# Attention weights of a graph layer: relu on ScalarE and one fused VectorE pass in place of two passes, and one broadcast row per head

## What is computed

```python
h = relu(layernorm(x))
ht = (h @ W).reshape(N, 4, 512).transpose(1, 0, 2)
src, dst = einsum("hnd,hd->hn", ht, a_src), einsum("hnd,hd->hn", ht, a_dst)
e = leaky_relu(src[:, :, None] + dst[:, None, :], 0.01) + adj_mat[None]
x = x + einsum("hij,hjd->hid", softmax(e, axis=-1), ht).mean(axis=0)
```

## Time and profile before

| | us |
|---|---|
| three runs | 2653.58, 2651.89, 2648.78 |
| median | 2651.89 |
| span of the profiled execution, first to last instruction | 2651.3 |
| PE busy in the span | 2503.3 |
| DVE busy in the span | 2309.6 |
| first matmul of the attention (L1226) starts at | 556.36 |

### The profile page before, as it was taken

The page is one execution under the profiler, slowest core; times in us unless marked ns, Lnnn a source line. Parts: engine busy times, 40 slices in busy tenths (PEclk is TensorE's granted clock), DMA queues, the critical chain, the costliest instruction groups (busy, mean ns, idle before and its releaser), DMA issues.

```text
span 2651.3 us, 46261 instructions
## 1 busy us (share of the span) xinstructions
PE 2503.3 (94%) x12326; PEld 1243.7 (47%) x12326; DVE 2309.6 (87%) x3220; ACT 1188.3 (45%) x1837; POOL 267.7 (10%) x206
## 2 busy tenths in 40 slices
PE   4899898759999999999999999999999999999997
PEld 1344346724444444444444444444444444444686
DVE  8998777479889998899888998888989899889796
ACT  5433344544444444454344553344544444444453
POOL 4105401310001000010001100010000100001000
PEclk8999998579999999999999999999999999999999
DMA  5443334420002100121001210022000210001000
GB/s 205 164 151 110 112 115 153 131 111 8 8 28 85 43 8 8 44 79 39 1 8 58 65 40 8 0 70 85 8 8 12 79 63 4 4 14 48 25 1 9
DMA packets 77246, 146.71 MB, mean 55 GB/s; under 512 B 4347, under 2 KB 12389, under 8 KB 76516
## 3 DMA queue, kind: packets, MB, share of 16 engines
q1 hardware_dynamic: 77156, 145.76, 17.2%
HBM read 131.99 MB, written 13.75 MB: 55 GB/s over the span
## 4 chain that ended last, share of the span: by engine, by line
PE 54%; DVE 17%; issue 6%; DVEq 3%; ACT 0%; ACTq 0%; POOLq 0%; POOL 0%
PE z_ps L1226 43%; PE o_ps L1250 10%; DVE t_reg L1140 5%; DVE ao_reg L1112 4%; DVE t_reg L1130 4%; DVE x_reg L1119 2%; DVE hl_reg L1097 1%; DVEq L1130 1%; PE c_ps L1241 1%; DVEq L1181 0%; DVE z_reg L1149 0%; DVEq L1119 0%; DVEq L1097 0%; ACT z_reg L1054 0%; DVEq L1128 0%
## 5 line engine op out<-in xcount | busy, mean ns | idle before, releaser
L1226 PE MATMUL z_ps<-hl_reg,h_reg 128*128 (+2 forms) x8736 | 1768.9, 365 | 55.9 <-DVE hl_reg L1097 40.2
L1226 PEld LDWEIGHTS z_ps<-hl_reg,h_reg 128*128 (+1 forms) x8736 | 855.2, 98 | 966.1 <-issue 44.7
L1042 ACT ACTIVATE hl_reg<-t_reg (+2 forms) x364 | 362.6, 996 | 870.4 <-PE z_ps L1226 485.8
L1130 DVE SCALAR_TENSOR_TENSOR t_reg<-ring_reg,vv,t_reg 128x512 f32 (+3 forms) x728 | 504.8, 736 | 7.7 <-issue 7.7
L1028 ACT ACTIVATE t_reg<-ring_reg,vv 128x512 f32 (+3 forms) x728 | 461.3, 681 | 29.4 <-DVE credits L1086 15.3
L1097 DVE TENSOR_TENSOR hl_reg<-t_reg,hl_reg (+2 forms) x364 | 417.4, 1147 | 31.8 <-ACT hl_reg L1042 31.1
L1140 DVE TENSOR_TENSOR t_reg<-t_reg,x_reg (+3 forms) x364 | 416.6, 1144 | 0.0
L1112 DVE TENSOR_TENSOR ao_reg<-ao_reg,t_reg 128x1024 f32<-128x1024 f32 (+1 forms) x336 | 384.7, 1145 | 0.0
L602 PE MATMUL z_ps<-t_reg,h_reg 128*128 (+2 forms) x1456 | 309.1, 373 | 53.5 <-DVE t_reg L384 47.2
L1250 PE MATMUL o_ps<-w_reg,z_reg 128*128 128x512 f16 x1248 | 273.9, 379 | 0.6 <-DVE z_reg L1149 0.6
L602 PEld LDWEIGHTS z_ps<-t_reg,h_reg 128*128 (+1 forms) x1456 | 144.6, 100 | 217.0 <-issue 61.3
(11 more groups left out here) (107 smaller groups left out, 855.8 us busy)
## 6 DMA issues: line engine op xcount, KB each, us to landing
ring_reg<-adjT_in SPq DMA_DIRECT2D x78, 512.0 KB, 3.7
x_reg<-adjT_in SPq DMA_DIRECT2D x78, 512.0 KB, 3.7
ring_reg<-rows_dram SPq DMA_DIRECT2D x24, 512.0 KB, 3.8
t_reg<-x_in SPq DMA_DIRECT2D x13, 512.0 KB, 4.2
x_dram<-x_reg SPq DMA_DIRECT2D x13, 512.0 KB, 4.7
ao_reg<-x_dram SPq DMA_DIRECT2D x6, 1024.0 KB, 5.6
out_dram<-ao_reg SPq DMA_DIRECT2D x6, 1024.0 KB
w_reg<-W_in SPq DMA_DIRECT2D x5, 1024.0 KB, 7.7
```

What stands on the lines that cost most here:

```text
L1042: nc.scalar.activation(hl_ring[:, g % HL_RING, 0, :, 0:W], t_ring[:, g % T_RING, :, 0:W], ACT.Copy).then_inc(hi_ready, 1)
L1130: nc.vector.scalar_tensor_tensor(out=tu, in0=u_bc[:, h, 1, 0:W], scalar=vv4[:, 1, h, bass.ds(p * 2 + u, 1)], in1=tu, op0=ALU.mult, op1=ALU ...
L1226: mm = nc.tensor.matmul(z_ps[:, k, 0:W], hk[hs], hl_ring[:, r, ps, u, 0:W], start=first and u == 0 and n == 0, stop=last and u == 1 and n ...
```

## The change

With C = U1 / U0 one value of i per head is enough: the weight is, up to a factor per i that cancels in the softmax, max(V1 C, V0) E = (relu(V1 C - V0) + V0) E. ACT does relu(V1 C - V0) with a per-partition scale and a per-partition bias, DVE adds V0 and multiplies by E in one scalar_tensor_tensor for each half. The pass L1140 is gone. The wait for the mask (`e_ready`) moves ahead of the first of these two. `p_ready` counts halves. `rows` has 5 rows in place of 9, and the broadcast load of a head is one row (256 KB) in place of two (512 KB). The factor 2^15 that the rows carried now goes into V0 and V1, so the rows no longer wait for a scaling pass on DVE (L886) before they are transposed; two small passes on V0, V1 and -V0 stand in its place.

```diff
@@ start of the stage
-                nc.vector.tensor_tensor(uu4[:, :, 0], qq3, lk3, ALU.subtract).then_inc(s_uarg, 1)
-                nc.vector.scalar_tensor_tensor(out=uu4[:, :, 1], in0=qq3, scalar=SLOPE, in1=lk3,
-                                               op0=ALU.mult, op1=ALU.subtract).then_inc(s_uarg, 1)
+                nc.vector.scalar_tensor_tensor(out=cc3, in0=qq3, scalar=SLOPE, in1=lk3,
+                                               op0=ALU.mult, op1=ALU.subtract).then_inc(s_carg, 1)
...
-                dve.wait_ge(s_uexp, 1)
-                nc.vector.tensor_scalar(rows[:, 0:2 * H * NT], rows[:, 0:2 * H * NT], PS, None,
-                                        ALU.mult).then_inc(s_rows, 1)
+                link(dve, nc.vector.tensor_scalar(vv[:, 0:2 * H * NT], vv[:, 0:2 * H * NT], PS, None, ALU.mult))
+                link(dve, nc.vector.tensor_scalar(vv4[:, 2], vv4[:, 0], -1.0, None, ALU.mult))
...
-                pe.wait_ge(s_rows, 1)
+                pe.wait_ge(s_cexp, 1)
+                pe.wait_ge(mt_red, len(max_groups))
@@ ACT, t1
                     for u in range(2):
-                        nc.scalar.activation(t_ring[:, g % T_RING, u, 0:W], u_bc[:, h, 0, 0:W], ACT.Copy,
-                                             scale=vv4[:, 0, h, bass.ds(p * 2 + u, 1)]).then_inc(t1_ready, 1)
+                        nc.scalar.activation(t_ring[:, g % T_RING, u, 0:W], c_bc[:, h, 0:W], ACT.Relu,
+                                             bias=vv4[:, 2, h, bass.ds(p * 2 + u, 1)],
+                                             scale=vv4[:, 1, h, bass.ds(p * 2 + u, 1)]).then_inc(t1_ready, 1)
@@ DVE, step
+                    if h == 0:
+                        dve.wait_ge(e_ready, b * PAIRS + p + 1)
                     for u in range(2):
                         dve.wait_ge(t1_ready, g * 2 + u + 1)
                         tu = t_ring[:, g % T_RING, u, 0:W]
-                        nc.vector.scalar_tensor_tensor(out=tu, in0=u_bc[:, h, 1, 0:W],
-                                                       scalar=vv4[:, 1, h, bass.ds(p * 2 + u, 1)], in1=tu,
-                                                       op0=ALU.mult, op1=ALU.max).then_inc(stt_done, 1)
+                        nc.vector.scalar_tensor_tensor(out=tu, in0=tu, scalar=vv4[:, 0, h, bass.ds(p * 2 + u, 1)],
+                                                       in1=e_blk[:, bass.ds(p * 2 + u, 1), 0:W]
+                                                       .rearrange("p o i -> p (o i)"),
+                                                       op0=ALU.add, op1=ALU.mult).then_inc(p_ready, 1)
                     if before:
                         lo_part(*before)
                     if e_of(b, h, p):
                         subtract_max(*e_of(b, h, p))
-                    dve.wait_ge(stt_done, g * 2 + 2)
-                    if h == 0:
-                        dve.wait_ge(e_ready, b * PAIRS + p + 1)
-                    nc.vector.tensor_tensor(tp, tp, e_blk[:, bass.ds(p * 2, 2), 0:W], ALU.mult).then_inc(p_ready, 1)
                     if before:
                         accumulate(*before)
```

More of the change, by code:

```diff
@@ L673, in gnn_kernel @@
         rows_out = sem("rows_out")
-        u_in = [sem(f"u_in{h}") for h in range(H)]
+        c_in = [sem(f"c_in{h}") for h in range(H)]
         e_in = [sem(f"e_in{p}") for p in range(PAIRS)]
@@ L736, in _ @@
                 load_max(sp, 0)
-                load_u(sp, 0, 0)
+                load_c(sp, 0, 0)
                 for p in range(EARLY, PAIRS):
@@ L740, in _ @@
                 for h in range(1, H):
-                    load_u(sp, 0, h)
+                    load_c(sp, 0, h)
                 load_x1(sp, 0)
@@ L783, in _ @@
                     nc.scalar.activation(vv4[:, q], dn3, ACT.Exp, scale=f).then_inc(s_vv, 1)
-                act.wait_ge(s_uarg, 2)
-                nc.scalar.activation(rows[:, 0:2 * H * NT], rows[:, 0:2 * H * NT], ACT.Exp).then_inc(s_uexp, 1)
+                act.wait_ge(s_carg, 1)
+                nc.scalar.activation(cc3, cc3, ACT.Exp).then_inc(s_cexp, 1)
                 for a in range(2):
```

51 lines of the change are left out of this document (24 added, 27 removed).

## The result

| | before | after |
|---|---|---|
| median, us | 2650.34 (4 runs, 2647.98 to 2653.58) | 2618.63 (4 runs, 2617.20 to 2618.89) |
| ratio, with its 95% interval | | 0.9879 [0.9865, 0.9893] |
| span of the profiled execution | 2651.3 | 2616.7 |
| DVE busy | 2309.6 | 1953.4 |
| ACT busy | 1188.3 | 1246.3 |

The kernel before has a fourth run here, 2647.98, beside the three listed above. The change makes the kernel 1.2% faster. 2616.5 was forecast, 2618.63 measured.

A forecast was written before the change was run, and what follows sets the result against it. PE bounds most stretches, so only its excess over its floor counts: 19.9 + 10.5 + 3.5 - 0.4 + 1.85 = 35.35 us off the span of 2651.3 gives 2616.0, forecast median 2616.5 us, range 2612 to 2629.

The forecast's parts named there:

- The bound: Full stretches of the second layer: PE's floor is 78.51 us; only its excess can be gained, 19.9 in the 23 intervals.
- Rival B: Masked steps stay slower than PE: 5.4 us per pair in block 0, 5.3 later; 2629 us; chance 0.14.
- D: Masked steps: relu and exponential do not share ACT's table, reloads of 1.28 us each; about 2710 us; chance 0.03.
- E: Gain handed back elsewhere, PE waiting as long for ACT's bank copies or POOL's tick; 2647 to 2652 us; chance 0.03.
- C: Start alone goes otherwise: barrier not earlier, or POOL's 8.2 us grows; 2619 to 2622 us; chance 0.08.
- The new pass: DVE's add-and-multiply passes cost as L1130, 1.32 us per pair; up to 0.5 more if like L842.
- The masked step: DVE's step with a mask subtraction falls from 5.94 to 4.80 us, 4.93 in block 0, below PE's 5.18.
- The first stretch: From the first attention matmul: falls from 85.68 us to a floor of 75.2, gaining 10.5.
- The half block: Its first stretch takes 48.57 us against a floor of 45.07; excess 3.5, of which 0.4 is kept back.
- The start: Up to the first attention matmul: 0.65 and 2.6 us less, 1.4 more for the longer order, together -1.85.
- so the tick moves with the barrier: Start of the stage: POOL's unexplained 8.2 us between barrier and first tick stay as they are.
- From span to median: Whole run: the median of the runs lies 0.6 us above the span, so 2616.0 becomes 2616.5.

The follow-up runs named there:

- e_long_exp: The kernel after, plus a 128x1024 copy on ACT ahead of each exponential of a mask; 2635.64 us, ratio 0.9939 against the kernel before.
- e_two_rows: The kernel after, with broadcast loads of two rows per head again (512 KB), the second row unused; 2617.59 us in one execution.
- e_pool_early: The kernel after, plus one POOL add of 128x1 right behind its partition_all_reduce; 2608.95 us, ratio 0.9846 against the kernel before.
- e_pass_all: The kernel after, plus a DVE pass of the old product's size into unused space in all 364 steps; 2638.32 us, ratio 0.9949 against before.
- e_pass_chain: The kernel after, plus a DVE pass of the old product's size in every step, with ACT's high part waiting for it; 2657.19 us, ratio 0.9994 against before.

## Why the prediction was right, point by point

**The bound: right.** Read as PE's excess over its floor, stretch by stretch, the gain came out as forecast: 19.9 of 19.9 in the intervals, from 356 us of DVE that went. Rival B needed masked steps longer than PE's pair in every block; they are 5.03 in the late ones. D needed table loads behind the start of the attention; the trace has 728 relu beside 91 exponentials there and no load (the stage's one is at 514.7). E is out by the size of the gain. C came true in its half: POOL's delay grew, by 1.0.

**The new pass: right.** It was costed as L1130, 1.32 for two; from start to next start it is 1.33 in block 0 (557.81 to 559.14 in the timeline). `t1` takes 800 ns, forecast 803, beside PE's work. Group of the kernel after by line and form:

```profile
L1025 ACT ACTIVATE t_reg<-ring_reg,vv 128x512 f32 x512 | 385.5, 800 | 50.3 <-DVE ao_reg L1110 41.9 <-issue 8.3
```

**The masked step: 4.80 and 4.93 forecast, 5.03 and, in block 0, 4.87 to 5.40 measured.** "The later masked steps hold the 4.80" missed that ACT's high part waits behind an exponential which waits for the subtraction in the same step. In block 0 the first steps, which are written out, are 4.87 (L1129 starts at 557.81 and 562.68); inside the hardware loop they are 5.40. The parts are the same; the handover from the exponential to the new pass grew from 0.03 (557.78 to 557.81, DVE having waited 0.52) to 0.45 (588.60 to 589.05), and the time from the subtraction's start to the exponential's by 0.1. Timeline of ACT and DVE in the kernel after, a written-out step and one in the loop:

```profile
556.72 1.06 ACT L1016 ACTIVATE x_reg<-x_reg 128x1024 f32<-128x1024 f32 x1 [1.46 <-DVE x_reg L1117]
...
557.81 1.41 DVE L1129 SCALAR_TENSOR_TENSOR t_reg<-t_reg,vv,x_reg 128x512 f32<-128x512 f32 x2 [0.52 <-ACT x_reg L1016]
...
562.68 1.42 DVE L1129 SCALAR_TENSOR_TENSOR t_reg<-t_reg,vv,x_reg 128x512 f32<-128x512 f32 x2
...
587.54 1.06 ACT L1016 ACTIVATE x_reg<-x_reg  x1 [1.98 <-DVE x_reg L1117]
...
589.05 1.41 DVE L1129 SCALAR_TENSOR_TENSOR t_reg<-t_reg,vv,x_reg  x2 [0.51 <-ACT x_reg L1016]
```

The cover was thus thinner than the prediction had it: the five full steps that the loop makes in block 0 are 0.2 above PE's pace and eat its lead, and the others have 0.15 and not 0.38 in hand. PE didn't wait, so the sum didn't feel it. `e_long_exp` did.

**The first stretch: floor mis-sized by 0.95.** 75.2 was forecast, 76.15 measured, with PE busy throughout. The first pair was taken as 7.04, the half-clock pair at a seam. Behind 30.9 us of waiting PE was granted the lower clock, 1.2 GHz, for about the first 5.4 us:

```profile
555.54:561.00 5.46, 5.46 (x13) 1.94 (x14) 4.94 (x8) 3.42 (x4) 0.00 (x0) 0.50 0.00 0
561.00:566.20 5.20, 5.20 (x25) 2.35 (x24) 5.20 (x7) 3.41 (x4) 0.00 (x0) 1.00 0.00 0
```

Half of that, 2.7, on top of 5.18 makes a first pair of 7.9, and 76.15 less 67.34 and 0.8 leaves 8.0. How long the low clock lasts differs from run to run at this place, and it doesn't follow the wait ahead of it: about 3.8 us before, behind 31.4 of waiting, and 3.6 in `e_two_rows`, behind 31.8. So the forecast's 7.04 would have fitted those two.

**The half block: 3.8 for 3.1.** The 0.4 kept back weren't needed, and 39.88 was not quite the floor: it is 39.60, which gave 0.6 more in the two stretches behind.

**The start: 1.85 forecast, 0.8 got.** The barrier came at 537.34, forecast 537.2, but the 2.6 from SP's loads are right by luck in their parts. The three `load_u` were to go from 4.31 to 2.2 and everything behind the first one to gain 0.7 at most. They took 3.55:

```profile
532.67 3.55 SPq L681 DMA_DIRECT2D ring_reg<-rows_dram  x3
```

The rest came from loads whose size didn't change: the eight of the adjacency 5.98 to 4.91, and that of x 1.31 to 0.61. The longer order behind the tick cost 1.3, forecast 1.4. The failed step is "so the tick moves with the barrier": POOL's 8.2 became 9.2. The prediction had named that as the sign by which its reading of the 8.2 would be wrong. The runs showed in its place a cost of POOL's first ordinary operation behind the all-reduce, that can be paid early (`e_pool_early`) and that, paid behind the barrier, isn't the same in every kernel (`e_two_rows`). The estimate from the Trainium skill's 6 us (GPSIMD Engine Reference, section Instruction dispatch) was a shorter delay behind the barrier with emptier queues; the delay went up. The DMA engines were in fact no emptier then: their busy share in the delay is 1.05 before, 1.01 after and 1.05 in `e_two_rows`.

**From span to median: 0.6 used, 1.9 measured.** A run's time is 1.7 to 2.1 above its own span in all runs here for which both are listed. For before the span of 2651.3 is listed with no time of its own; by the same 1.7 to 2.1 it belongs to a run of 2653.0 to 2653.4, near its slowest (2653.58), so that its span lay close to the median by chance. That is 1.3 of the 2.1 us by which the forecast missed; the span itself missed by 0.7 (2616.0 against 2616.7).

**What the prediction said too simply** is the cause. It counted the removed product as DVE's time alone. By the time from the first matmul on, the amount of work alone brings back 20.4 of the 33.7 us gained (2094.9 to 2061.2); in the product's old place, between the weights and the high part, the same pass brings back 38.0. By the ratios the kernel after is 0.0121 below before, `e_pass_all` brings back 0.0070 of that, and `e_pass_chain` 0.0115, with 1 inside its interval. Both measures say that the work alone is some 60% of the gain and the old place all of it; the exact share is not pinned down. Why `e_pass_chain` is 4.3 above the trace of before no run shows: the two are from different chips, on which before itself has medians 8 us apart (2650.34 and 2658.42). The forecast was safe from all this only because it took the whole excess of PE as the gain.

Two things stay open: why POOL's delay behind the barrier is 7.5, 8.2 or 9.2 in three kernels that there differ in the size of their loads and, before against the other two, in what ACT and DVE do; and what the later high part alone would cost behind masked steps of the present length.

## What to carry to other kernels

Where one engine is at its floor in most stretches, sum its excess over that floor and stop there: work removed elsewhere is worth no more. To find what a removed step was worth, put an idle one back, first where it only takes time and then where it also holds up the next engine; here it cost 12 us (by the ratios) to 17.6 us (by the traces) more in the second place than in the first. Behind a special instruction on GpSimd issue an ordinary one at once, on nothing, if a later one is awaited.
